# A graph layer with residual and layer norm: the first 1024 nodes' two halves take turns, group by group

## The chip, the cores and the metric

The kernel runs on one core of one Trainium2 chip. The metric is the device time of one execution in microseconds (us), the median of three runs. The core has engines that run side by side and meet through semaphores: TensorE (PE, matmuls; PEld are its weight loads), VectorE (DVE), ScalarE (ACT), GpSimd (POOL) and SyncE (SP), which here only starts transfers. ACT can start transfers as well, in a queue of its own.

## The reference

```python
support = x @ weight                                # x 4096 x 256, weight 256 x 256
h = (1.0 - ts) * support + ts * (adj @ support)     # adj 4096 x 4096, ts = t[0]
y = layernorm(x + h)                                # over the 256 features, eps 1e-5
```

Everything is float32. The kernel computes z = ts * (adj @ x) + (1 - ts) * x first and then z @ weight, which is the same sum with the large product taken first.

## The kernel before

The output nodes are cut into 8 chunks of 512 (`WIDE`). For one chunk the kernel needs all 32 blocks of 128 rows of x (`x_hi`, `x_lo`, 128 x 256 each, kept in SBUF once loaded) against the 32 blocks of that chunk's transposed adjacency (128 x 512 each, 256 KB). Four adjacency blocks form a group of 1 MB (`GROUP`), so a chunk has 8 groups; a group lives in one of four slots (`RING`) of `a_raw`, `a_hi` and `a_lo`.

Float32 products are made from two rounded parts. For each adjacency piece ACT writes the rounded high part `a_hi` (L209 for the first pieces, L216 for whole groups), DVE writes the rest `a_lo = a_raw - a_hi` (L370, L299), and PE then multiplies hi x hi, hi x lo and lo x hi (L449, L450, L451), for each of the two halves of the features (`k`): six matmuls of 512 columns for a block, 24 for a group. The blocks of x are split the same way: the first four by DVE (`x_hi`, L358) and POOL (`x_lo`, L273), the others by ACT (L203) and DVE (L364). The sums of a chunk stand in two PSUM banks `agg[c % 2]`.

While x is still coming, chunk 0 runs in small pieces (`PIECES`: first block, number of blocks), in the order in which they arrive: piece p is x blocks and adjacency blocks together. ACT's queue starts the first four adjacency pieces (L197), SP's queue the first five x pieces (L126), then x and adjacency in turn (L126, L131), and from block 16 on whole groups (L140). SP starts the load of a group into a slot when DVE has made `a_lo` of what stood there; ACT writes `a_hi` of a group when PE has used up the slot (`a_used`). So loading and splitting run up to four groups ahead of PE, and each engine follows the same written order of groups.

PE's own order is: 8 matmuls on zeros (`WARM`, L539), the first block (`first_piece`, L457 to L465), the pieces of chunk 0, its groups 4 to 7, and then for each next chunk group 0, the projection of the chunk before (`project`, 24 matmuls of 256 columns), and groups 1 to 7. `make_z` and `z_high` turn a finished chunk's `agg` into the operands `z_hi`, `z_lo` of that projection; they stand in DVE's and ACT's order ahead of the fourth group of the next chunk, and `layernorm` behind the fifth. The last chunk has a finish of its own (`project_last`).

## Time and profile before

| | us |
|---|---|
| median of 3 runs | 388.32 (387.94 to 388.32) |
| the profiled execution | 388.26 |
| its span, first to last instruction | 386.4 |
| PE busy / DVE busy / ACT busy / POOL busy | 377.9 / 226.7 / 145.5 / 20.7 |

The profiled execution took 388.26 us, of which 386.4 lie between its first and last instruction. Busy times are sums of an engine's instructions; a busy PE is not PE at its peak, since matmuls overlap. The distance from one matmul's start to the next is the figure to read. In the rows, `x8` is a number of instructions in one line, and in the timeline the brackets at the end give the idle time ahead of an instruction and what ended it.

### The profile page before, as it was taken

The numbers are of one execution on the slowest core, as the hardware profiler recorded it, in microseconds if no ns is written. First come the engines' busy times: TensorE is split into PE (matmuls) and PEld (weight loads), VectorE is DVE, ScalarE is ACT, GpSimd is POOL, SyncE is SP. The second block draws the span as 40 slices with busy tenths as digits, with TensorE's granted clock in tenths as the row PEclk, the third lists the DMA queues.
The fourth block names the chain that finished last, engine by engine and source line by source line (L and its number), as shares of the span: only waits on it lengthen the run. The fifth ranks groups of instructions, "written<-read, shape, count | busy, mean of one in ns | idle before, by whom it ended". The sixth has DMA issues, their size and how long they took to land.

```text
span 386.4 us, 4238 instructions
## 1 busy us (share of the span) xinstructions
PE 377.9 (98%) x1744; PEld 314.7 (81%) x1744; DVE 226.7 (59%) x292; ACT 145.5 (38%) x111; POOL 20.7 (5%) x20
## 2 busy tenths in 40 slices
PE   7999999999999999999999999999999999999993
PEld 5787888888888888888888888888888888888883
DVE  3978789454693356744576446763378444693115
ACT  4777553323523324233424325233333233523002
POOL 3200220010000100001000100001000010000000
PEclk9999999999999999999999999999999999999999
DMA  7999996566556565565646656647556565420001
GB/s 244 390 415 418 420 412 229 191 245 265 165 205 236 216 236 202 170 266 217 246 164 220 222 196 260 219 163 271 175 207 219 177 257 215 145 102 31 0 0 55
DMA packets 19251, 83.89 MB, mean 217 GB/s; under 512 B 1952, under 2 KB 7072, under 8 KB 11552
## 3 DMA queue, kind: packets, MB, share of 16 engines
...
q14 instruction: 6, 0.05, 0.0%
HBM read 79.43 MB, written 4.19 MB: 216 GB/s over the span
## 4 chain that ended last, share of the span: by engine, by line
PE 91%; DMA 5%; DVE 3%; ACT 1%; ACTq 0%; issue 0%; SPq 0%
PE agg L449 28%; PE agg L450 28%; PE agg L451 28%; DMA a_raw<-in_adjT 5%; PE out_ps L507 2%; PE out_ps L506 2%; PE out_ps L505 2%; DVE a_lo L370 1%; DVE a_lo L299 1%; ACT a_hi L216 0%; DVE x_lo L364 0%; DVE stats L419 0%; ACT x_raw L262 0%; ACTq L197 0%; ACT a_hi L209 0%
## 5 line engine op out<-in xcount | busy, mean ns | idle before, releaser
L299 DVE TENSOR_TENSOR a_lo<-a_raw,a_hi 128x2048 fp32r<-128x2048 f32 x60 | 140.8, 2348 | 123.2 <-ACT a_hi L216 123.2
L449 PE MATMUL agg<-a_hi,x_hi 128*128 128x512 f32 x510 | 199.0, 390 | 0.5 <-DVE a_lo L299 0.3
L450 PE MATMUL agg<-a_lo,x_hi 128*128 128x512 f32 x510 | 198.5, 389 | 0.0
L451 PE MATMUL agg<-a_hi,x_lo 128*128 128x512 f32 x510 | 198.4, 389 | 0.0
L216 ACT ACTIVATE a_hi<-a_raw 128x2048 fp32r<-128x2048 f32 x60 | 114.9, 1915 | 136.8 <-PE agg L451 127.7
L449 PEld LDWEIGHTS agg<-a_hi,x_hi 128*128 128x128 f32 x510 | 95.7, 188 | 21.8 <-DVE a_lo L370 1.3
L451 PEld LDWEIGHTS agg<-a_hi,x_lo 128*128 128x128 f32 x510 | 95.7, 188 | 20.1
L450 PEld LDWEIGHTS agg<-a_lo,x_hi 128*128 128x128 f32 x510 | 95.8, 188 | 19.4
L278 POOL TENSOR_TENSOR xt<-xt,omt_col 128x1024 f32<-128x1024 f32 x8 | 15.7, 1957 | 287.7 <-DMA xt<-in_xT 287.7
L223 ACT ACTIVATE z_hi<-z 128x512 fp32r<-128x512 f32 x14 | 8.9, 634 | 26.2 <-DVE z L312 26.2
L227 ACT ACTIVATE std<-var_eps 128x4 f32<-128x4 f32 x7 | 1.4, 205 | 42.1 <-DVE var_eps L335 42.1
L507 PE MATMUL out_ps<-w_hi,z_lo 128*128 128x256 f32 x56 | 15.8, 283 | 0.0
L506 PE MATMUL out_ps<-w_lo,z_hi 128*128 128x256 f32 x56 | 15.8, 283 | 0.0
L505 PE MATMUL out_ps<-w_hi,z_hi 128*128 128x256 f32 x56 | 15.8, 282 | 0.0
L370 DVE TENSOR_TENSOR a_lo<-a_raw,a_hi 128x512 fp32r<-128x512 f32 (+1 forms) x11 | 10.7, 972 | 3.7 <-ACT a_hi L209 3.3
L330 DVE BATCH_NORM_STATS2 stats<-x_raw 128x6 f32<-128x256 f32 x28 | 12.0, 428 | 1.0
L312 DVE SCALAR_TENSOR_TENSOR z<-agg,t_col,xt 128x512 f32<-128x512 f32 x14 | 10.4, 746 | 2.9 <-PE agg L451 2.9
L327 DVE TENSOR_TENSOR x_raw<-out_ps,rows 128x256 f32<-128x256 f32 x28 | 11.5, 410 | 0.0
L209 ACT ACTIVATE a_hi<-a_raw 128x512 fp32r<-128x512 f32 (+1 forms) x11 | 9.1, 828 | 5.4 <-DMA a_raw<-in_adjT 5.3
L505 PEld LDWEIGHTS out_ps<-w_hi,z_hi 128*128 128x128 f32 x56 | 10.7, 191 | 0.3
L506 PEld LDWEIGHTS out_ps<-w_lo,z_hi 128*128 128x128 f32 x56 | 10.7, 191 | 0.3
L507 PEld LDWEIGHTS out_ps<-w_hi,z_lo 128*128 128x128 f32 x56 | 10.7, 191 | 0.0
...
## 6 DMA issues: line engine op xcount, KB each, us to landing
...
x_raw<-in_x SPq DMA_DIRECT2D x5, 256.0 KB, 7.4
a_raw<-in_adjT ACTq DMA_DIRECT2D x4, 256.0 KB, 5.4
```

The lines of the kernel that those rows point to most:

```text
L216: nc.scalar.activation(a_hi[:, slot], a_raw[:, slot], ACT.Copy).then_inc(a_hi_ready[slot], 1)
L278: nc.gpsimd.tensor_tensor(xt[:, c % 2], xt[:, c % 2], omt_col[:, :].unsqueeze(2).broadcast_to([P, KT, WIDE]), ALU.mult).then_inc(xt_scaled, 1)
L299: nc.vector.tensor_tensor(a_lo[:, slot], a_raw[:, slot], a_hi[:, slot].bitcast(f32), ALU.subtract).then_inc(a_lo_ready[slot], 1)
L327: nc.vector.tensor_tensor(y_tile(i), out_ps[i][:, 0:feats], rows[:, c % 2, i], ALU.add).then_inc(y_ready[i], 1)
L330: nc.vector.bn_stats(stats[:, i], y_tile(i)).then_inc(stats_ready, 1)
L370: nc.vector.tensor_tensor(a_lo[:, j // GROUP, j % GROUP:j % GROUP + n], a_raw[:, j // GROUP, j % GROUP:j % GROUP + n], a_hi[:, j // GROUP, ...
L449: nc.tensor.matmul(bank, x_hi[:, j, cols], a_hi[:, slot, b], start=first, stop=False)
L450: nc.tensor.matmul(bank, x_hi[:, j, cols], a_lo[:, slot, b], start=False, stop=False)
L451: return nc.tensor.matmul(bank, x_lo[:, j, cols], a_hi[:, slot, b], start=False, stop=last)
L505: nc.tensor.matmul(dst, z_hi[:, k, cols], w_hi[:, k], start=(k == 0), stop=False)
L506: nc.tensor.matmul(dst, z_hi[:, k, cols], w_lo[:, k], start=False, stop=False)
L507: done = nc.tensor.matmul(dst, z_lo[:, k, cols], w_hi[:, k], start=False, stop=(k == KT - 1))
```

## The change

The order of the groups becomes one sequence n. For chunks 0 and 1 it alternates: n = 0 is chunk 0 group 0, n = 1 is chunk 1 group 0, n = 2 is chunk 0 group 1, and so on to n = 15; from n = 16 on it is chunk by chunk as before. The slot is n % 4. A group of x is thus used for two groups of adjacency in a row, and x is spread over the first 16 groups of work where it was spread over the first 8.

The pieces are cut anew. x has 12 pieces (`X_PIECES`: first block, count). The first four slots' adjacency has 13 pieces (`A_PIECES`: slot, first block, count, first and last column); slots 0 and 1 come block by block in turn, slots 2 and 3 in turns of two blocks. The first adjacency block comes as two transfers of 256 columns. ACT's queue starts pieces 0 to 3 (two halves, chunk 1's first block, chunk 0's second); SP's queue starts x 0, x 1, piece 4 (chunk 1's second block), x 2, pieces 5 and 6, x 3, and so on, with t and the weight behind all pieces. Splitting keeps to its engines: ACT `a_hi`, DVE `a_lo`, the first four x blocks by DVE and POOL.

PE runs 5 matmuls on zeros where it ran 8, and two more on zeros that write the banks of chunk 0; the first block follows as 12 matmuls of 256 columns where it was 6 of 512. The projection of chunk 0 comes behind n = 15, that of chunk 1 behind n = 18, the others where they were. `make_z`, `z_high`, `root` and `layernorm` keep their distances to the end of their chunk from chunk 2 on; for chunk 0 `make_z` stands ahead of n = 18 and `layernorm` behind n = 19, for chunk 1 ahead of n = 19 and behind n = 22. Loads of `xt` come two groups later, those of `rows` too from chunk 2 on, and the two that belong to chunk 0 come behind n = 8 and n = 10.

```diff
@@ -9,9 +9,12 @@
 GROUP = 4
 RING = 4
 X_RING = 3
-WARM = 8
-PIECES = ((0, 1), (1, 1), (2, 1), (3, 1), (4, 1), (5, 1), (6, 2), (8, 2), (10, 2), (12, 2), (14, 2),
-          (16, 4), (20, 4), (24, 4), (28, 4))
+WARM = 5
+X_PIECES = ((0, 1), (1, 1), (2, 1), (3, 1), (4, 2), (6, 2), (8, 4), (12, 4), (16, 4), (20, 4), (24, 4), (28, 4))
+A_PIECES = ((0, 0, 1, 0, 256), (0, 0, 1, 256, 512), (1, 0, 1, 0, 512),
+            (0, 1, 1, 0, 512), (1, 1, 1, 0, 512), (0, 2, 1, 0, 512), (1, 2, 1, 0, 512),
+            (0, 3, 1, 0, 512), (1, 3, 1, 0, 512),
+            (2, 0, 2, 0, 512), (3, 0, 2, 0, 512), (2, 2, 2, 0, 512), (3, 2, 2, 0, 512))
 EPS = 1e-5
 
 
@@ -27,11 +30,26 @@
     TILES = WIDE // P
     assert GROUPS == 2 * RING and KT == 2 and TILES == GROUP
 
-    EARLY = sum(first < GROUP for first, _ in PIECES)
-    RING_PIECES = sum(first < RING * GROUP for first, _ in PIECES)
-
-    def piece_after(blocks):
-        return sum(first < blocks for first, _ in PIECES)
+    EARLY = sum(first < GROUP for first, _ in X_PIECES)
+    SECOND = sum(first < 2 * GROUP for first, _ in X_PIECES)
+    A_EARLY = sum(slot < 2 for slot, *_ in A_PIECES)
+    TURNS = CHUNKS * GROUPS
+
+    def seq(c, g):
+        return 2 * g + c if c < 2 else c * GROUPS + g
+
+    def chunk_group(n):
+        return (n % 2, n // 2) if n < 2 * GROUPS else (n // GROUPS, n % GROUPS)
+
+    def x_after(blocks):
+        return sum(first < blocks for first, _ in X_PIECES)
+
+    def a_after(slot):
+        return max(q for q, piece in enumerate(A_PIECES) if piece[0] == slot) + 1
+
+    LAST = [seq(c, GROUPS - 1) for c in range(CHUNKS)]
+    PROJECT_AFTER = [LAST[c] + (3 if c == 1 else 1) for c in range(CHUNKS)]
+    NORM_AFTER = [PROJECT_AFTER[c] + 4 for c in range(CHUNKS)]
...
@@ -158,29 +184,37 @@
 
             load_x(0)
             load_x(1)
-            for p in range(2, len(PIECES)):
-                load_x(p)
-                if p >= 4 and p < RING_PIECES:
-                    load_adj_piece(p)
-                if p == 5:
-                    sp.dma_start(t_col[:, :], t.partition_broadcast(P)).then_inc(t_loaded, 16)
-                if p == 8:
-                    sp.dma_start(w_raw[:, :, :], W.rearrange("(k p) n -> p k n", p=P)).then_inc(w_loaded, 16)
-                if p >= RING_PIECES:
-                    load_adj(0, PIECES[p][0] // GROUP)
-            load_adj(1, 0)
-            load_xt(0)
-            load_rows(0)
-            for c in range(1, CHUNKS):
-                for g in range(1, GROUPS):
-                    load_adj(c, g)
-                    if g == 2:
-                        load_xt(c)
-                    if g == 5 and c + 1 < CHUNKS:
-                        load_rows(c)
-                if c + 1 < CHUNKS:
-                    load_adj(c + 1, 0)
-                store(c - 1)
+            load_adj_piece(4)
+            load_x(2)
+            load_adj_piece(5)
+            load_adj_piece(6)
+            load_x(3)
+            load_adj_piece(7)
+            load_adj_piece(8)
+            load_x(4)
+            load_adj_piece(9)
+            load_adj_piece(10)
+            load_x(5)
+            load_adj_piece(11)
+            load_adj_piece(12)
+            sp.dma_start(t_col[:, :], t.partition_broadcast(P)).then_inc(t_loaded, 16)
+            sp.dma_start(w_raw[:, :, :], W.rearrange("(k p) n -> p k n", p=P)).then_inc(w_loaded, 16)
+            for n in range(RING, TURNS):
+                c, g = chunk_group(n)
+                if c == 0:
+                    load_x(x_after(g * GROUP))
+                load_adj(n)
+                if c < 2 and g == 4:
+                    load_xt(c)
+                if c < 2 and g == 5:
+                    load_rows(c)
+                if c >= 2 and g == 4:
+                    load_xt(c)
+                if c >= 2 and g == 7 and c + 1 < CHUNKS:
+                    load_rows(c)
+                for d in range(CHUNKS - 1):
+                    if n == min(NORM_AFTER[d] + RING, TURNS - 1):
+                        store(d)
             c = CHUNKS - 1
             for i in range(2):
...
-                    if g == RING - 1:
-                        make_z(c - 1)
-                    a_low(c, g)
-                    if g == RING:
-                        layernorm(c - 1)
+            x_high(0)
+            a_low_piece(0)
+            a_low_piece(1)
+            x_high(1)
+            a_low_piece(2)
+            x_high(2)
+            a_low_piece(3)
+            a_low_piece(4)
+            x_high(3)
+            for q in range(5, A_EARLY):
+                a_low_piece(q)
+            for p in range(EARLY, SECOND):
+                x_low(p)
+                for q in (A_EARLY + 2 * (p - EARLY), A_EARLY + 2 * (p - EARLY) + 1):
+                    a_low_piece(q)
+            dve.wait_ge(w_hi_ready, 1)
+            nc.vector.tensor_tensor(w_lo[:, :, :], w_raw[:, :, :], w_hi[:, :, :].bitcast(f32), ALU.subtract
+                                    ).then_inc(w_lo_ready, 1)
+            dve.wait_ge(t_loaded, 16)
+            nc.vector.tensor_scalar(omt_col[:, :], t_col[:, :], -1.0, 1.0, ALU.mult, ALU.add).then_inc(omt_ready, 1)
+            for n in range(RING, TURNS):
+                c, g = chunk_group(n)
+                if c == 0:
+                    x_low(x_after(g * GROUP))
+                for d in range(CHUNKS - 1):
+                    if n == LAST[d] + RING:
+                        make_z(d)
+                a_low(n)
+                if n == 2 * GROUPS:
+                    dve.wait_ge(x0_lo_ready, EARLY)
+                    dve.wait_ge(x_lo_ready, len(X_PIECES) - EARLY)
+                for d in range(CHUNKS - 1):
+                    if n == NORM_AFTER[d]:
+                        layernorm(d)
             c = CHUNKS - 1
             dve.wait_ge(xt_scaled, c + 1)
...
+            def first_block():
+                def half(k, w, a, q):
+                    lo, hi = A_PIECES[q][3:]
+                    nc.tensor.matmul(agg[0][k][:, lo:hi], w[:, 0, k * P:(k + 1) * P], a_part(a, q)[:, 0],
+                                     start=False, stop=False)
+
                 pe.wait_ge(x0_hi_ready, 1)
-                pe.wait_ge(a0_hi_ready, 1)
-                for k in range(KT):
-                    nc.tensor.matmul(agg[0][k][:, :], x_hi[:, 0, k * P:(k + 1) * P], a_hi[:, 0, 0],
-                                     start=True, stop=False)
-                pe.wait_ge(a0_lo_ready, 1)
-                for k in range(KT):
-                    nc.tensor.matmul(agg[0][k][:, :], x_hi[:, 0, k * P:(k + 1) * P], a_lo[:, 0, 0],
-                                     start=False, stop=False)
-                pe.wait_ge(x0_lo_ready, 1)
-                for k in range(KT):
-                    nc.tensor.matmul(agg[0][k][:, :], x_lo[:, 0, k * P:(k + 1) * P], a_hi[:, 0, 0],
-                                     start=False, stop=False)
-
-            def piece(p):
-                j, n = PIECES[p]
-                pe.wait_ge(a0_lo_ready, p + 1)
-                if p < EARLY:
-                    pe.wait_ge(x0_lo_ready, p + 1)
+                for q in range(2):
+                    pe.wait_ge(a0_hi_ready, q + 1)
+                    for k in range(KT):
+                        half(k, x_hi, a_hi, q)
+                for q in range(2):
+                    pe.wait_ge(a0_lo_ready, q + 1)
+                    for k in range(KT):
+                        half(k, x_hi, a_lo, q)
+                    if q == 0:
+                        pe.wait_ge(x0_lo_ready, 1)
+                    for k in range(KT):
+                        half(k, x_lo, a_hi, q)
...
+
+            def piece(q):
+                slot, first, count, _, _ = A_PIECES[q]
+                c, g = chunk_group(slot)
+                pe.wait_ge(a0_lo_ready, q + 1)
+                if g == 0:
+                    pe.wait_ge(x0_lo_ready, first + 1)
                 else:
-                    pe.wait_ge(x_lo_ready, p - EARLY + 1)
-                for b in range(j, j + n):
+                    pe.wait_ge(x_lo_ready, x_after(g * GROUP + first + count) - EARLY)
+                for b in range(first, first + count):
+                    j = g * GROUP + b
                     for k in range(KT):
-                        done = products(0, b // GROUP, b, b % GROUP, k, False, False)
-                if (j + n) % GROUP == 0:
...
@@ -537,17 +581,18 @@
             pe.wait_ge(zeros_ready, 1)
             for _ in range(WARM):
                 nc.tensor.matmul(out_ps[0][:, :], z_hi[:, 0, 0:P], z_hi[:, 0], start=True, stop=True)
-            first_piece()
-            for p in range(1, RING_PIECES):
-                piece(p)
-            for g in range(RING, GROUPS):
-                group(0, g)
-            pe.wait_ge(w_lo_ready, 1)
-            for c in range(1, CHUNKS):
-                group(c, 0)
-                project(c - 1)
-                for g in range(1, GROUPS):
-                    group(c, g)
+            for k in range(KT):
+                nc.tensor.matmul(agg[0][k][:, :], z_hi[:, 0, 0:P], z_hi[:, 0], start=True, stop=False)
+            first_block()
+            for q in range(2, len(A_PIECES)):
+                piece(q)
+            for n in range(RING, TURNS):
+                group(n)
+                for d in range(CHUNKS - 1):
+                    if n == PROJECT_AFTER[d]:
+                        if d == 0:
+                            pe.wait_ge(w_lo_ready, 1)
+                        project(d)
             project_last()
 
 ```

ACT's loop has the same order as DVE's, with `a_high_piece`, `x_high`, `z_high` and `root` in the places of `a_low_piece`, `x_low`, `make_z` and `layernorm`; SP's `load_adj(n)` waits for the `a_lo` of the slot's last use as before.

## Rows read from the trace of the kernel before

**Rows 1.** The page: busy time of the engines, and GB/s in 40 slices.
```profile
PE 377.9 (98%) x1744; PEld 314.7 (81%) x1744; DVE 226.7 (59%) x292; ACT 145.5 (38%) x111; POOL 20.7 (5%) x20
...
GB/s 244 390 415 418 420 412 229 191 245 265 165 205 236 216 236 202 170 266 217 246 164 220 222 196 260 219 163 271 175 207 219 177 257 215 145 102 31 0 0 55
```
**Rows 2.** Waits of PE over the span: us in total, times, longest.
```profile
PE agg L457 <- ACT a_hi L209: 0.4, 1, 0.4
PE agg L449 <- DVE a_lo L299: 0.3, 1, 0.3
PE agg L449 <- DVE a_lo L370: 0.2, 1, 0.2
```
**Rows 3.** Timeline of PE at the start: start us, us, engine, line.
```profile
1.38 3.78 PE L539 MATMUL out_ps<-z_hi 128*128 128x512 f32 x8 [1.38 <-POOL z_hi L282]
5.56 1.09 PE L457 MATMUL agg<-a_hi,x_hi 128*128 128x512 f32 x2 [0.40 <-ACT a_hi L209]
6.49 0.63 PE L461 MATMUL agg<-a_lo,x_hi 128*128 128x512 f32 x2
...
7.76 0.50 PE L449 MATMUL agg<-a_hi,x_hi 128*128 128x512 f32 x1 [0.18 <-DVE a_lo L370]
8.10 0.40 PE L450 MATMUL agg<-a_lo,x_hi 128*128 128x512 f32 x1
...
9.33 0.50 PE L449 MATMUL agg<-a_hi,x_hi 128*128 128x512 f32 x1
...
18.05 0.39 PE L449 MATMUL agg<-a_hi,x_hi 128*128 128x512 f32 x1
...
28.25 0.39 PE L449 MATMUL agg<-a_hi,x_hi 128*128 128x512 f32 x1
...
29.42 0.50 PE L449 MATMUL agg<-a_hi,x_hi 128*128 128x512 f32 x1 [0.33 <-DVE a_lo L299]
```
**Rows 4.** Timeline of PE at the end of the last group.
```profile
376.26 0.28 PE L517 MATMUL out_ps<-w_hi,z_hi 128*128 128x256 f32 x1
376.38 0.28 PE L518 MATMUL out_ps<-w_lo,z_hi 128*128 128x256 f32 x1
```
**Rows 5.** Timeline of ACT: the pieces that waited, and the first whole group.
```profile
6.17 0.63 ACT L209 ACTIVATE a_hi<-a_raw 128x512 fp32r<-128x512 f32 x1 [0.76 <-DMA a_raw<-in_adjT]
7.67 0.63 ACT L209 ACTIVATE a_hi<-a_raw 128x512 fp32r<-128x512 f32 x1 [0.87 <-DMA a_raw<-in_adjT]
8.74 0.63 ACT L209 ACTIVATE a_hi<-a_raw 128x512 fp32r<-128x512 f32 x1 [0.44 <-DMA a_raw<-in_adjT]
...
25.12 1.92 ACT L216 ACTIVATE a_hi<-a_raw 128x2048 fp32r<-128x2048 f32 x1 [0.91 <-DMA a_raw<-in_adjT]
```
**Rows 6.** Timeline of DVE: the second and the third block's `a_lo`.
```profile
6.83 0.88 DVE L370 TENSOR_TENSOR a_lo<-a_raw,a_hi 128x512 fp32r<-128x512 f32 x1 [0.49 <-ACT a_hi L209]
...
8.33 0.94 DVE L370 TENSOR_TENSOR a_lo<-a_raw,a_hi 128x512 fp32r<-128x512 f32 x1 [0.42 <-ACT a_hi L209]
```
**Rows 7.** Timeline of the DMA queues: the starts of the first transfers.
```profile
0.80 2.28 SPq L126 DMA_DIRECT2D x_raw<-in_x  x5
0.81 1.85 ACTq L197 DMA_DIRECT2D a_raw<-in_adjT  x4
```
**Rows 8.** Transfers started at 1.24 us: KB each, us to landing.
```profile
a_raw<-in_adjT ACTq DMA_DIRECT2D x1, 256.0 KB, 4.9
x_raw<-in_x SPq DMA_DIRECT2D x1, 128.0 KB, 4.3
```
**Rows 9.** The same view, transfers started at 1.71 and 1.72 us.
```profile
a_raw<-in_adjT ACTq DMA_DIRECT2D x1, 256.0 KB, 5.9
x_raw<-in_x SPq DMA_DIRECT2D x1, 128.0 KB, 5.7
```
**Rows 10.** The page: groups of instructions, busy and mean ns, idle before.
```profile
L299 DVE TENSOR_TENSOR a_lo<-a_raw,a_hi 128x2048 fp32r<-128x2048 f32 x60 | 140.8, 2348 | 123.2 <-ACT a_hi L216 123.2
...
L312 DVE SCALAR_TENSOR_TENSOR z<-agg,t_col,xt 128x512 f32<-128x512 f32 x14 | 10.4, 746 | 2.9 <-PE agg L451 2.9
```

177 lines of the change are left out of this document (79 added, 98 removed).

## The prediction

> **What bounds the kernel now.** I read the page first: PE is busy 377.9 of 386.4 us, DVE 226.7 and ACT 145.5 [rows 1]. The waits of PE come next, and they are nearly nothing: three short ones on the product banks, 0.9 us together [rows 2]. So the kernel is a stream of matmuls, and the question is how dense the stream is. The timeline answers that. From 18.05 to 28.25 us 45 matmuls of 512 columns start, 0.2267 us apart [rows 3]; two of 256 columns start 0.12 us apart [rows 4]. From the first whole group at 29.42 us to the end of the last at 376.26 us there are 1440 of the wide ones and seven projections of 24 narrow ones: 1440 x 0.2267 + 168 x 0.12 = 346.6 us, and the rows give 346.84 [rows 3, 4]. Nothing is lost there. What can be won lies ahead of 29.42 us: from 5.56 us on 96 matmuls run, 21.76 us of work in 23.86 us, so 2.1 us are lost [rows 3]. Half of it goes before 9.33 us (12 matmuls, 2.72 us, in 3.77 us) and half behind (84 matmuls, 19.04 us, in 20.09 us). Ahead of 5.56 us PE waits for its first data.
>
> Both losses come from loading. The ACT rows say that each of the first pieces was split the moment it landed, at 6.17, 7.67 and 8.74 us [rows 5], and the first whole group at 25.12 us, when the queues moved 390 to 420 GB/s [rows 1, 5]; its matmuls were 0.49 us late, since the one before would have let them start at 28.93.
>
> **The later loss goes.** After the change a block of x and two adjacency blocks, 640 KB, feed twelve matmuls (2.72 us) where 768 KB did. Up to n = 4 the queues carry eight x blocks fewer, 1 MB, at 415 GB/s 2.5 us: the first whole group should land at 22.6 us for 25.12 now. ACT's 1.92 us [rows 5] and DVE's 2.35 us [rows 10] put it ready near 27 us with x's own splitting between, two us ahead of PE. DVE needs at most 0.94 us for a block's `a_lo` [rows 6] against PE's 1.36 us, so the splitting keeps ahead too. I take the 1.05 us behind the third block as gone but for 0.05 us.
>
> **The first block.** The half piece is a smaller transfer and should land some tenths earlier than the 256 KB one, and its `a_hi` is half the work. The first matmul comes near 4.9 us for 5.56. The zeros are 7 matmuls for 8, at the 0.45 us that those rows show (1.38 us on, eight in 3.78 us, the last one 0.63 long) they end in time [rows 3]. Twelve half matmuls cost 12 x 0.12 = 1.44 us for 6 x 0.2267 = 1.36: 0.08 us more, and twice that while the clock is still low. None of it counts if the block behind it is late, and it is: the first block should be through by 7 us.
>
> **The second and third piece** decide. They are the third and fourth transfer of ACT's queue (chunk 1's first block, chunk 0's second). ACT's queue holds 512 KB up to the second piece now and then, so by its own contents nothing changes. But the two queues share the engines. The transfers started at 1.24 us land 4.3 (x, 128 KB) and 4.9 us (adjacency, 256 KB) later, those of 1.71 and 1.72 us 5.7 and 5.9 us later [rows 8, 9]: the k-th transfer of one queue lands with the k-th of the other, though one is twice as large. All are 128 rows, one for each partition. Landed with the second pair (6.14 us) are 768 KB, with the third (7.62 us) 1152, with the fourth (8.70 us) 1536 [rows 5, 8, 9]; the starts are 0.46 us apart and bound nothing [rows 7]. After the change chunk 1's first block is third in its queue, and beside it SP's third is a whole adjacency block, not x. Together with the halves and x 0 and x 1, that is 1024 KB: 6.14 + 256/384 x 1.48 = 7.13 us. Chunk 0's second block is fourth, with 1408 KB: 7.62 + 256/384 x 1.08 = 8.34 us.
>
> The ends for the first of them: 6.14 us, if ACT's queue keeps its bytes per us, and 7.62 us, if the third pair lands when the third pair did. I take 7.13, between them by the bytes moved. From landing to the first matmul it was 7.76 - 6.14 = 1.62 us and 9.33 - 7.62 = 1.71 us [rows 3, 8, 9]. So PE starts chunk 1's first block at 8.75 us, a restart costs 0.11 us (8.10 - 7.76 = 0.34 for 0.23 us) [rows 3], and it is done at 8.75 + 1.36 + 0.11 = 10.22 us. The next is ready at 8.34 + 1.7 = 10.04 us, in time. At 10.22 us 12 blocks' worth of matmuls are done as at 9.33 us now, 0.89 us later, and behind it stand 84.
>
> **The rule weighed.** The landings in pairs are the row; a byte share of each queue would give other times. The Trainium skill (DMA: Bandwidth & Descriptors, Queues, rings and completion order) says that each DMA engine takes the queues in turn, a packet at a time. By strict turns the third transfer lands with the third pair, at 7.62 us. This speaks against the change, which puts larger transfers beside the ones that PE waits for. It is the second rival below.
>
> **The rest of the stream.** The projection of chunk 0 comes behind n = 15. Its operands need the end of n = 14, then `z` 0.75 us [rows 10], `z_hi` (0.63, the same shape as in rows 5) and `z_lo` (under 0.94, rows 6): 2.3 us beside 5.44 us of matmuls. Chunk 1's `z_hi` and `z_lo` wait for that projection (2.9 us behind n = 15), and behind them in ACT's and DVE's queues stand the splits of n = 19: ready at 2.9 + 1.3 + 0.9 + 1.9 + 2.35 = 9.4 us, needed after three groups and a projection, 22.1 us. Then `layernorm`: DVE's busy time without L299 is 85.9 us [rows 1, 10], at most 12.3 us for each of seven, so n = 20 is ready by 9.4 + 12.3 + 2.35 = 24.1 us, needed at 27.6. On SP's queue `xt` and `rows` move by two groups, with data that are wanted a chunk's end later. I count all this at nothing; without that cover a projection would cost its wait of up to 2.3 us. The last chunk is untouched.
>
> **Sum.** 10.22 + 84 x 0.2267 + 0.05 = 29.31 us for the start of the 97th block matmul, where it was 29.42: 0.1 us earlier. The profiled execution is 388.26 us, 0.06 under the median of 388.32; 388.26 - 0.1 gives **388.1 us** (388.16, the 0.05 for gaps being the most I allow). One loss goes and almost the same loss comes in ahead of it.
>
> **Rivals.** First, the pieces land by their place in ACT's queue: 6.14 and 7.62 us. PE starts them at 7.76 and 9.33 as now and only the later loss goes: 9.33 + 19.04 + 0.15 = 28.5 us, 0.9 us gained, **387.3 us**. For it speaks that early on the queues moved less than later (244 GB/s in the first slice for 415 [rows 1]), so room may be left for the larger rows; against it the landing in pairs.
>
> Second, strict turns: 7.62 us for chunk 1's first block. Start 9.33, done 10.8, 29.9 us, 0.5 us lost: **388.7 us**. Within 0.2% of now.
>
> Third, the clock, on the slower side. The matmuls on zeros start 0.45 us apart, those from 6.49 us on 0.23 us: PE went from its level of 1.2 GHz to that of 2.4 GHz around the first block, having run without a pause for 3.8 us and then with one of 0.4 us [rows 3]. After the change it has seven zeros, single half matmuls with waits between, and then stands still from about 7 to 8.75 us. If it is at the low level when chunk 1's first block begins, each matmul costs 0.22 us more: six cost 1.3 us, **389.4 us**, and this decides as soon as four or more run so. Against it: the pause of 0.4 us and the ones ahead of 7.76 and 9.33 us didn't bring it down now.
>
> Fourth, the turn of chunk 0 and 1 stalls PE behind n = 15 for over a us after all: 389 us and more.
>
> **How the numbers follow.** Forecast 0.40, by place 0.25, strict turns 0.18, clock 0.12, turn 0.05. A difference of 0.2% (0.78 us) is about what a measurement of this kernel can tell. Faster by more: most of the first rival and a tail of the forecast, 0.26. Slower by more: clock and turn, less their mild cases, 0.15. Within: 0.59. The range of 8 in 10 reaches from 387.2 (first rival, with 0.1 us of an earlier landing) to 389.0, with the second rival in and most of the clock out.
>
> **What would show it.** PE's first matmul near 4.9 us and the first block done by 7; then an idle of 1.5 to 2 us that ends with DVE's `a_lo` of chunk 1's first block, near 8.7 us; ACT's third piece starting at 7.1 us on a DMA. From about 10.2 us no idle of PE to the end, and the first whole group ready 2 us early. I am wrong on landing if ACT's third piece starts at 6.2 or at 7.7 us; on the clock if matmuls behind 8.7 us start over 0.4 us apart; on the cover if PE waits at the first narrow matmuls near 94 us.

## The result and the profile after

The changed kernel takes 390.65 us, the median of 10 runs (388.50 to 391.82), against 388.32 us for the kernel before, measured beside it (10 runs, 387.89 to 389.32). The ratio is 1.0051, with a 95% interval of 1.0036 to 1.0065: slower by 0.5%, and outside the predicted range, which ended at 389.0. The profiled execution took 390.79 us with a span of 389.1; that of before took 388.26 with a span of 386.4.

First the page of the changed kernel: its sums, and the GB/s of the 40 slices.

```profile
PE 379.9 (98%) x1749; PEld 317.7 (82%) x1749; DVE 224.5 (58%) x291; ACT 144.9 (37%) x110; POOL 21.4 (5%) x20
...
GB/s 227 368 416 417 416 411 255 184 168 222 142 252 277 170 263 188 245 216 201 212 238 207 187 254 217 224 207 202 227 166 271 175 202 271 145 101 26 0 0 56
```

PE is busy 2.0 us longer than before [rows 1], though there is hardly more to compute: the matmuls themselves have become slower somewhere. The first two slices carry less than before (227 for 244 and 368 for 390 GB/s). The waits of PE in the changed kernel (us in total, times, longest) don't name the loss:

```profile
PE out_ps L583 <- POOL z_hi L313: 1.4, 1, 1.4
PE agg L485 <- DVE a_lo L399: 0.6, 1, 0.6
PE agg L492 <- ACT a_hi L239: 0.6, 1, 0.6
```

The first of them, for the zeros at the very start, both kernels have. The two others are 1.2 us together, and before had 0.9 [rows 2]. The timeline of PE in the changed kernel (start us, us, engine, line) shows what the list of waits can't:

```profile
1.38 2.50 PE L583 MATMUL out_ps<-z_hi 128*128 128x512 f32 x5 [1.38 <-POOL z_hi L313]
3.68 1.05 PE L585 MATMUL agg<-z_hi 128*128 128x512 f32 x2
4.56 0.76 PE L492 MATMUL agg<-a_hi,x_hi 128*128 128x256 f32 x2
5.95 0.80 PE L492 MATMUL agg<-a_hi,x_hi 128*128 128x256 f32 x2 [0.62 <-ACT a_hi L239]
...
7.83 0.63 PE L492 MATMUL agg<-a_hi,x_lo 128*128 128x256 f32 x2
9.09 0.80 PE L485 MATMUL agg<-a_hi,x_hi 128*128 128x512 f32 x1 [0.63 <-DVE a_lo L399]
9.68 0.63 PE L486 MATMUL agg<-a_lo,x_hi 128*128 128x512 f32 x1
...
13.52 0.55 PE L486 MATMUL agg<-a_lo,x_hi 128*128 128x512 f32 x1
13.90 0.39 PE L487 MATMUL agg<-a_hi,x_lo 128*128 128x512 f32 x1
...
31.84 0.39 PE L485 MATMUL agg<-a_hi,x_hi 128*128 128x512 f32 x1
...
378.55 0.28 PE L561 MATMUL out_ps<-w_hi,z_hi 128*128 128x256 f32 x1
```

Wide matmuls that depend on nothing but the one before start 0.43 us apart up to 13.52 us, and 0.23 us apart from 13.90 on: PE stays at its level of 1.2 GHz for four microseconds of real work. In the kernel before the change to 0.23 us came with the first block, at about 6.5 us [rows 3]. From 9.09 to 13.90 us eleven matmuls take 4.81 us; at 0.2267 us, with the 0.11 us of a restart, they would take 2.60. That is **2.2 us, lost to the clock**. Behind it nothing is lost: the 97th block matmul starts at 31.84 us (29.42 before), the last group ends at 378.55, where the narrow matmuls behind it begin (376.26 before [rows 4]).

So 2.3 of the 2.7 us by which the span grew arise ahead of 31.84 us. The other 0.4 us lie behind the last group: from 378.55 us to the end of the span it is 10.5 us, from 376.26 us it was 10.1. The computing there is the same; the last wait of the kernel, SP's on the store of the result, is 2.4 us for 2.0.

The start of ACT in the changed kernel shows when the pieces landed, and so why PE had to wait:

```profile
4.00 0.42 ACT L239 ACTIVATE a_hi<-a_raw 128x256 fp32r<-128x256 f32 x1
5.48 0.42 ACT L239 ACTIVATE a_hi<-a_raw 128x256 fp32r<-128x256 f32 x1 [1.06 <-DMA a_raw<-in_adjT]
7.68 0.63 ACT L239 ACTIVATE a_hi<-a_raw 128x512 fp32r<-128x512 f32 x1 [1.78 <-DMA a_raw<-in_adjT]
8.68 2.19 ACT L239 ACTIVATE a_hi<-a_raw 128x512 fp32r<-128x512 f32 x4 [0.37 <-DMA a_raw<-in_adjT]
...
24.99 1.92 ACT L245 ACTIVATE a_hi<-a_raw 128x2048 fp32r<-128x2048 f32 x1 [1.44 <-DMA a_raw<-in_adjT]
```

The second half lands at 5.5 us, chunk 1's first block at 7.63 us, chunk 0's second at 8.6. Before, the next block was there at 6.14, the third at 7.62 [rows 5, 8, 9], and the whole first one by 4.78 us, as ACT's row of before shows:

```profile
4.78 0.63 ACT L209 ACTIVATE a_hi<-a_raw 128x512 fp32r<-128x512 f32 x1 [0.81 <-DMA a_raw<-in_adjT]
```

So the second half of the block came 0.7 us later than the whole block had. The third transfers of the two queues, as the view of transfers has them (KB each, us from issue to landing; they started at 1.71 and 1.73 us), land within 0.2 us of each other:

```profile
a_raw<-in_adjT SPq DMA_DIRECT2D x1, 256.0 KB, 5.8
a_raw<-in_adjT ACTq DMA_DIRECT2D x1, 256.0 KB, 5.9
```

### The profile page after: what moved, and what is told of

It is laid out like the page before. It is cut to its first block, busy times and chain, and to the rows that moved or that the text cites. A ratio compares the mean times of both kernels' runs of the same rounds, so it can differ in the third digit from the quotient of the medians.

```text
span 389.1 us, 4247 instructions
## 1 busy us (share of the span) xinstructions
PE 379.9 (98%) x1749; PEld 317.7 (82%) x1749; DVE 224.5 (58%) x291; ACT 144.9 (37%) x110; POOL 21.4 (5%) x20
## 3 DMA queue, kind: packets, MB, share of 16 engines
q10 hardware_dynamic: 864, 1.05, 1.1%
## 4 chain that ended last, share of the span: by engine, by line
PE 96%; DMA 2%; DVE 1%; ACT 1%; ACTq 0%; issue 0%
PE agg L485 30%; PE agg L486 30%; PE agg L487 30%; PE out_ps L551 2%; PE out_ps L550 2%; PE out_ps L549 2%; DMA a_raw<-in_adjT 2%; DVE stats L455 0%; ACT x_raw L293 0%; ACTq L230 0%; DVE a_lo L399 0%; ACT a_hi L239 0%; PE out_ps L561 0%; PE out_ps L563 0%; PE out_ps L562 0%; PE out_ps L567 0%
## 5 line engine op out<-in xcount | busy, mean ns | idle before, releaser
L330 DVE TENSOR_TENSOR a_lo<-a_raw,a_hi 128x2048 fp32r<-128x2048 f32 x60 | 138.6, 2311 | 124.3 <-ACT a_hi L245 124.3
L485 PE MATMUL agg<-a_hi,x_hi 128*128 128x512 f32 x510 | 199.6, 391 | 0.6 <-DVE a_lo L399 0.6
L486 PE MATMUL agg<-a_lo,x_hi 128*128 128x512 f32 x510 | 199.4, 391 | 0.0
L487 PE MATMUL agg<-a_hi,x_lo 128*128 128x512 f32 x510 | 199.1, 390 | 0.0
L245 ACT ACTIVATE a_hi<-a_raw 128x2048 fp32r<-128x2048 f32 x60 | 114.8, 1915 | 137.6 <-PE agg L487 134.1
L485 PEld LDWEIGHTS agg<-a_hi,x_hi 128*128 128x128 f32 x510 | 96.3, 189 | 20.7 <-DVE a_lo L399 0.9
L487 PEld LDWEIGHTS agg<-a_hi,x_lo 128*128 128x128 f32 x510 | 96.3, 189 | 20.3
L486 PEld LDWEIGHTS agg<-a_lo,x_hi 128*128 128x128 f32 x510 | 96.4, 189 | 19.6
L309 POOL TENSOR_TENSOR xt<-xt,omt_col 128x1024 f32<-128x1024 f32 x8 | 16.7, 2089 | 298.5 <-DMA xt<-in_xT 298.5
L399 DVE TENSOR_TENSOR a_lo<-a_raw,a_hi 128x512 fp32r<-128x512 f32 (+2 forms) x13 | 11.5, 903 | 5.9 <-ACT a_hi L239 5.5
L343 DVE SCALAR_TENSOR_TENSOR z<-agg,t_col,xt 128x512 f32<-128x512 f32 x14 | 10.4, 747 | 2.8 <-PE agg L487 2.8
L239 ACT ACTIVATE a_hi<-a_raw 128x512 fp32r<-128x512 f32 (+2 forms) x13 | 9.2, 727 | 7.2 <-DMA a_raw<-in_adjT 7.2
L349 DVE TENSOR_TENSOR z_lo<-z,z_hi 128x512 fp32r<-128x512 f32 x14 | 9.5, 687 | 2.8 <-ACT z_hi L252 2.2
L550 PEld LDWEIGHTS out_ps<-w_lo,z_hi 128*128 128x128 f32 x56 | 10.7, 191 | 0.3
L549 PEld LDWEIGHTS out_ps<-w_hi,z_hi 128*128 128x128 f32 x56 | 10.7, 191 | 0.3
## 6 DMA issues: line engine op xcount, KB each, us to landing
a_raw<-in_adjT SPq DMA_DIRECT2D x5, 256.0 KB, 6.8
x_raw<-in_x SPq DMA_DIRECT2D x4, 128.0 KB, 4.7
```

The costliest lines, as they stand in the source:

```text
L245: nc.scalar.activation(a_hi[:, slot], a_raw[:, slot], ACT.Copy).then_inc(a_hi_ready[slot], 1)
L309: nc.gpsimd.tensor_tensor(xt[:, c % 2], xt[:, c % 2], omt_col[:, :].unsqueeze(2).broadcast_to([P, KT, WIDE]), ALU.mult).then_inc(xt_scaled, 1)
L330: nc.vector.tensor_tensor(a_lo[:, slot], a_raw[:, slot], a_hi[:, slot].bitcast(f32), ALU.subtract).then_inc(a_lo_ready[slot], 1)
L399: nc.vector.tensor_tensor(a_part(a_lo, q), a_part(a_raw, q), a_part(a_hi, q).bitcast(f32), ALU.subtract).then_inc(a0_lo_ready, 1)
L485: nc.tensor.matmul(bank, x_hi[:, j, cols], a_hi[:, slot, b], start=first, stop=False)
L486: nc.tensor.matmul(bank, x_hi[:, j, cols], a_lo[:, slot, b], start=False, stop=False)
```

## The experiments

All times are medians in us, and each ratio is against the kernel before on the same chip in the same session. The kernel before had 388.28 (29 runs) beside the first four, 388.50 (25) beside the next four, 388.31 (27) beside the four after those and 388.57 (23) beside the last four.

| label | kernel | us (lowest to highest, runs) | ratio, 95% interval |
|---|---|---|---|
| e1_fill | after, zeros in both pauses | 389.05 (388.50 to 389.30, 11) | 1.0015, 1.0006 to 1.0023 |
| e2_before_w5 | before, 5 zeros for 8 | 388.61 (387.81 to 389.95, 12) | 1.0008, 0.9996 to 1.0019 |
| e3_x_first | after, all early x ahead on SP | 390.22 (388.77 to 390.68, 6) | 1.0042, 1.0026 to 1.0058 |
| e4_whole | after, first block whole | 388.44 (387.91 to 389.20, 12) | 1.0003, 0.9994 to 1.0011 |
| e5_warm8 | after, 8 zeros for 5 | 389.18 (388.38 to 391.13, 11) | 1.0019, 1.0008 to 1.0031 |
| e6_swap_fill | e1, chunk 1's first block by SP | 389.69 (389.04 to 390.91, 7) | 1.0035, 1.0022 to 1.0047 |
| e7_before_fill | before, two more zeros | 388.39 (388.06 to 388.97, 11) | 0.9999, 0.9990 to 1.0008 |
| e8_before_halves | before, first block in halves | 390.23 (389.44 to 391.67, 6) | 1.0050, 1.0032 to 1.0069 |
| e9_layout | after, adjacency stored in order of use | 391.92 (391.19 to 392.08, 4) | 1.0086, 1.0073 to 1.0100 |
| e10_before_far | before, two early blocks from far away | 388.52 (387.88 to 388.80, 11) | 1.0001, 0.9992 to 1.0009 |
| e11_whole_fill | e4 and 8 zeros | 388.26 (387.70 to 389.64, 11) | 1.0003, 0.9993 to 1.0013 |
| e12_whole_fill_layout | e11, stored in order of use | 387.52 (387.33 to 387.98, 11) | 0.9977, 0.9968 to 0.9986 |
| e13_halves_fill_layout | e1, stored in order of use | 389.64 (389.42 to 390.10, 5) | 1.0032, 1.0020 to 1.0044 |
| e15_after_again | after, once more | 389.43 (388.74 to 390.68, 7) | 1.0027, 1.0014 to 1.0039 |
| e16_best_again | e12, once more | 387.54 (387.20 to 388.15, 10) | 0.9981, 0.9972 to 0.9990 |
| e17_whole_layout | e12 with 5 zeros | 388.47 (387.69 to 389.65, 11) | 1.0002, 0.9991 to 1.0013 |

### The clock: zeros in the pauses

Theory: PE's two pauses, behind the first half and behind the first block, keep it at 1.2 GHz. The edit leaves every transfer and every wait and lets PE multiply zeros into an idle bank where it would stand still.

```diff
 pe.wait_ge(a0_hi_ready, q + 1)
 for k in range(KT):
     half(k, x_hi, a_hi, q)
+if q == 0:
+    fill(2)       # two 512-column matmuls on zeros into out_ps[0]
 ...
 first_block()
+fill(2)
```

> The changed kernel with four more matmuls on zeros, 512 columns each: two behind the first half's matmuls and two behind the first block, in the two pauses of 0.6 us that PE has there; nothing else differs. Theory (clock): these pauses keep PE at its low level until 13.8 us, which costs 2.2 us; filled, the spacing goes from 0.43 to 0.23 us before 9 us, the 97th block matmul starts near 29.6 us for 31.84, and the time is 388.4 to 388.8 us. Rival (landing): the time is lost because chunk 1's first block lands 1.5 us later than the second piece of the kernel before did; fillers don't change that and the time stays at 390.5 us or rises by up to 0.4.

Measured 389.05 us, ratio 1.0015, for 1.0051 of after and 1.0027 of its second series (below). PE at the start of this kernel:

```profile
6.55 0.50 PE L496 MATMUL agg<-a_hi,x_hi 128*128 128x256 f32 x2 [0.38 <-ACT a_hi L239]
6.89 0.40 PE L496 MATMUL agg<-a_lo,x_hi 128*128 128x256 f32 x2
...
9.32 0.50 PE L485 MATMUL agg<-a_hi,x_hi 128*128 128x512 f32 x1 [0.84 <-DVE a_lo L399]
9.66 0.40 PE L486 MATMUL agg<-a_lo,x_hi 128*128 128x512 f32 x1
```

The level comes up at about 6.5 us, as before, and the matmuls of chunk 1's first block start 0.23 us apart, 0.84 us of pause notwithstanding. The kernel does four matmuls more and ends earlier. But it still stands above the kernel before, and not by its clock: the last group ends 0.5 us later than in before (376.77 us), and from there to the end it is 10.7 us for 10.1.

The change also takes three of the eight zeros away at the start. Given back in after:

```diff
-WARM = 5
+WARM = 8
```

> The changed kernel with 8 matmuls on zeros ahead of everything, as the kernel before had, for 5; nothing else differs. They and the two that write the banks end near 5.7 us, so the pause of 0.6 us ahead of the second half is closed, the one of 0.6 to 0.8 us ahead of chunk 1's first block stays. Theory (clock): closing the first pause is enough for the spacing to fall to 0.23 us before 8 us, as with the fillers in both pauses: 388.8 to 389.3 us. Rival (both pauses count): 390 to 390.7 us, with the low level past 10 us.

389.18 us, ratio 1.0019, and the level is up by 7.6 us: the same as with the fillers. The other way round, the kernel before with five zeros:

> The kernel before with 5 matmuls on zeros for 8, so that PE pauses for 1.2 us more ahead of its first block; loads and splits are untouched. Theory (clock): the pause alone keeps the low level beyond 9 us, each of the matmuls until it rises costs 0.2 us more, the time is 389.5 to 391 us and differs between runs by over 1 us. Rival (landing): no load or split depends on these matmuls, so the time stays at 388.3 us.

388.61 us, where I had expected 389.5 or more. PE pauses 1.8 us ahead of 5.68 us and then stays at 0.43 us until 10.9 us, and yet little is lost. The third block's matmuls start 1.6 us later than in before (10.94 for 9.33), the first whole group's only 0.6 us later (30.04 for 29.42): the 1.05 us that PE loses there in before, waiting for loads, are gone, so most of the slow matmuls run inside waiting time. The number of zeros alone is not what made after slow. And more zeros don't help the kernel before:

```diff
-WARM = 8
+WARM = 9
 ...
 first_piece()
+nc.tensor.matmul(out_ps[0][:, :], z_hi[:, 0, 0:P], z_hi[:, 0], start=True, stop=True)
```

> The kernel before with 9 matmuls on zeros for 8 and one more behind the first block, in its pauses of 0.4 and 0.2 us; nothing else differs. Theory (clock): the kernel before too loses some of its time to a low level in part of its executions, which is why its times reach from 387.7 to 388.9 us; without a pause the level rises early in all of them: median 388.0 us and a spread under 0.6 us. Rival (its spread comes from loading): 388.3 to 388.5 us with the same spread.

388.39 us, the same as before.

After itself came out at 388.5 to 391.8 us, a wider spread than the kernel before has. So it was profiled once more, with nothing changed:

> The changed kernel itself, unchanged, for a second profile. Theory (a property of the order of the transfers): chunk 1's first block again lands between 7.5 and 8 us, the queues again move under 250 GB/s from 4 to 6 us, PE pauses twice for over 0.5 us before 9.5 us, and the low level lasts past 9 us: 390.0 to 391 us. Rival (the first profile was a chance): landing near 7.1 us and over 270 GB/s.

This profiled execution took 389.15 us. Its PE:

```profile
5.91 0.80 PE L492 MATMUL agg<-a_hi,x_hi 128*128 128x256 f32 x2 [0.60 <-ACT a_hi L239]
...
8.74 0.79 PE L485 MATMUL agg<-a_hi,x_hi 128*128 128x512 f32 x1 [0.33 <-DVE a_lo L399]
9.33 0.63 PE L486 MATMUL agg<-a_lo,x_hi 128*128 128x512 f32 x1
9.76 0.62 PE L487 MATMUL agg<-a_hi,x_lo 128*128 128x512 f32 x1
10.19 0.43 PE L485 MATMUL agg<-a_hi,x_hi 128*128 128x512 f32 x1
10.46 0.40 PE L486 MATMUL agg<-a_lo,x_hi 128*128 128x512 f32 x1
```

The same kernel and the same pause behind the first half, a shorter one ahead of chunk 1's first block (0.33 us for 0.63), and the level is up at 10.2 us and not at 13.8. Three matmuls are slow where eleven were: from 8.74 to 10.19 us 1.45 us for 3 x 0.2267 + 0.11 = 0.79, so 0.7 us lost to the clock and not 2.2. The last group ends at 376.69 us, 1.86 earlier than in the first execution: 1.5 us of it are the clock's and 0.35 the earlier start of chunk 1's first block. What the change costs depends on the execution.

### The halves alone

Two kernels take the halves apart from the rest of the change. In after, the first block whole again (one piece, six 512-column matmuls; ACT's queue carries the same three blocks in three transfers, SP's queue is unchanged, and the chunks still take turns):

```diff
-A_PIECES = ((0, 0, 1, 0, 256), (0, 0, 1, 256, 512), (1, 0, 1, 0, 512),
+A_PIECES = ((0, 0, 1, 0, 512), (1, 0, 1, 0, 512),
 ...
```

> The changed kernel with the first adjacency block as one transfer of 256 KB and six matmuls of 512 columns, so that chunk 1's first block is the second transfer of ACT's queue; SP's queue and the turns of the chunks are kept. Theory (turns): chunk 1's first block lands near 6.2 us and chunk 0's second near 7.7 us, as the second and third piece of the kernel before; the first block starts near 5.5 us, chunk 1's at 7.8 us, and the pauses ahead of them add up to under 1.3 us with 7 zeros ending at 4.5 us. With the clock up by 8 us the time is 387.4 to 388 us, below the kernel before; if the clock stays low as in the changed kernel it is 389.5 to 390. Rival (the turns of the chunks themselves cost the 2.3 us): 390.5 us.

388.44 us: no difference from before, though PE pauses 1.47 us ahead of 6.20 us and is slow until 10.1 us. Chunk 1's first block, second in ACT's queue again, landed at 7.0 us, not near 6.2 as expected. With eight zeros as well:

> The changed kernel with the first adjacency block whole, and 8 zeros for 5, so that PE has no pause of 1.5 us ahead of it. Against the same kernel with 5 zeros (388.44 us): theory (clock) the low level ends by 8 us for 10.1, three or four matmuls of the stream that sets the end are 0.2 us shorter each: 387.7 to 388.1 us. Rival (the loads bind up to 10 us): 388.4 us.

388.26 us. The turns of the two chunks, with all that they move, come out even. They lose 1.0 us in front (the 13th block matmul starts at 10.35 us for 9.33) and win 0.85 us behind it (from there to the 97th it is 19.24 us for 20.09). And the halves put into the kernel before, with nothing else of the change:

```diff
-for p in range(4):
+act.dma_start(a_raw[:, 0, 0:1, 0:256], adjT[0, :, 0:1, 0:256]).then_inc(half_loaded, 16)
+act.dma_start(a_raw[:, 0, 0:1, 256:512], adjT[0, :, 0:1, 256:512]).then_inc(a0_loaded[0], 16)
+for p in range(1, 4):
     load_adj_piece(p)
 ...
```

> The kernel before with one part of the change alone: the first adjacency block as two transfers of 256 columns, split in two and multiplied as twelve matmuls of 256 columns behind two that write zeros (6 + 2 zeros in all, for 8). Theory (the halves take a place in ACT's queue): the second piece lands as the third transfer, at 7.3 to 7.7 us for 6.15, the pauses grow, and the time is 389 to 390.5 us. Rival (only the turns of the chunks and SP's larger transfers delay it): the second piece lands at 6.2 us and the time is 388.0 to 388.4 us.

390.23 us, 1.7 us more than before, between the 2.3 us of after's first series and the 0.9 us of its second. One part of the change, put in alone, costs about what the whole does, but not by the path that I had expected. The profile is of the slowest of its six executions, 391.67 us. The second piece, now the third transfer of ACT's queue, was to land at 7.3 to 7.7 us. ACT in it, at that piece:

```profile
6.50 0.63 ACT L218 ACTIVATE a_hi<-a_raw 128x512 fp32r<-128x512 f32 x1 [1.09 <-DMA a_raw<-in_adjT]
```

That is 0.3 us later than in before [rows 5], and PE starts on it at 7.90 us for 7.76. ACT again, at the x blocks ahead of the first whole group and at that group:

```profile
23.10 1.06 ACT L204 ACTIVATE x_hi<-x_raw 128x1024 fp32r<-128x1024 f32 x1 [0.21 <-DMA x_raw<-in_x]
...
26.99 1.92 ACT L225 ACTIVATE a_hi<-a_raw 128x2048 fp32r<-128x2048 f32 x1 [2.30 <-DMA a_raw<-in_adjT]
```

and PE, from the last early piece on:

```profile
28.96 0.39 PE L469 MATMUL agg<-a_hi,x_lo 128*128 128x512 f32 x1
31.28 0.64 PE L467 MATMUL agg<-a_hi,x_hi 128*128 128x512 f32 x1 [1.93 <-DVE a_lo L310]
31.72 0.63 PE L468 MATMUL agg<-a_lo,x_hi 128*128 128x512 f32 x1
...
34.71 0.49 PE L469 MATMUL agg<-a_hi,x_lo 128*128 128x512 f32 x1
35.04 0.39 PE L467 MATMUL agg<-a_hi,x_hi 128*128 128x512 f32 x1
```

The pieces near the start came nearly in time (the third block's matmuls begin at 9.73 us for 9.33). What is late is the first whole group, at 26.99 us where it was 25.12 [rows 5], and PE pauses 1.9 us for it. Then the clock adds to it: behind that pause eight matmuls start 0.43 us apart, 8 x 0.2 = 1.6 us more.

Of the 1.9 us, 0.5 are there already at the x blocks (23.10 us for 22.63). The other 1.4 arise in the group's own load: it lands 3.9 us behind them, in before 2.5. The view of transfers of e8 from 23.5 to 24.9 us names the one thing in that load that before doesn't have there, a packet of a queue of its own (packets, MB, share of the 16 engines):

```profile
q8 instruction: 1, 0.02, 4.9%
```

In before such a packet falls between 26 and 26.5 us, in the second whole group's load, and that group is there 4.8 us behind the first (29.91 for 25.12 us). That the packet holds the load up is likely, and not shown: e10 below has one at the same time, and its second group comes 3.9 us behind the first. So the profiled execution shows a late group and the clock, and what half a block at the front of ACT's queue costs by itself stays open in this kernel; the other five executions, 389.44 us at the least, have no profile.

### The landing of chunk 1's first block

Theory after e1: it lands late since SP's queue has a whole adjacency block beside it where there was x. The edit puts all early x blocks ahead on SP.

```diff
 load_x(1)
+load_x(2)
+load_x(3)
 load_adj_piece(4)
-load_x(2)
 load_adj_piece(5)
 load_adj_piece(6)
-load_x(3)
```

> The changed kernel with SP's queue in the order x 0, x 1, x 2, x 3, then pieces 4, 5 and 6; nothing else differs. Theory (turns): the third transfer of one queue lands with the third of the other, so chunk 1's first block has 128 KB less beside it and lands near 7.2 us for 7.65, chunk 0's second block 0.3 us earlier than now; PE starts at 8.6 us for 9.09. Its pauses get shorter, so the clock may rise earlier: 388.5 to 390.3 us. Rival (place in its own queue): landing at 7.65 us as before and 390.6 us.

390.22 us, and chunk 1's first block landed at 7.8 us, not earlier than 7.63. With 128 KB beside it for 256 the third transfer of ACT's queue gained nothing, against the theory of bytes. But the pair came apart: x 2, the third transfer of SP's queue, landed at 6.9 us, 0.9 us ahead. And the queues moved 139 GB/s from 4 to 6 us for 210, so the run isn't a clean test of either. If the place in the queue counts, the block has to get another place:

```diff
 load_x(0)
+load_adj_piece(2)
 load_x(1)
 ...
-for q in range(4):
+for q in (0, 1, 3):      # ACT's queue; with the fillers of e1
```

> The changed kernel with the four fillers, and chunk 1's first block started by SP as its second transfer for ACT as its third; ACT's queue has the halves and chunk 0's second block. Theory (place in its queue and what stands ahead in both): chunk 1's first block lands at 6.0 to 6.8 us for 7.9, PE starts it at 7.7 to 8.4 us for 9.3, chunk 0's second block lands at 7.6 us and is the next to wait for: 387.4 to 388.2 us. Rival (the queues as a whole deliver too little by then, in whatever order): landing past 7.3 us and 388.8 to 389.2 us.

389.69 us. The block landed at 6.3 us, in the second place of SP's queue, 1.6 us earlier than in e1 (7.9). But x 1, moved back by a place, slipped from 5.6 to 8.8 us, the second half from 6.1 to 6.5, chunk 0's second block from 8.9 to 9.3. PE started chunk 1's first block at 9.81 us, and that isn't the block's landing any more. DVE in this run:

```profile
8.87 0.29 DVE L390 CAST x_hi<-x_raw 128x256 fp32r<-128x256 f32 x1 [1.47 <-DMA x_raw<-in_x]
9.07 0.68 DVE L400 TENSOR_TENSOR a_lo<-a_raw,a_hi 128x512 fp32r<-128x512 f32 x1
```

In DVE's written order `x_high(1)` stands ahead of the block's `a_lo`, so DVE waited for x 1, which this block doesn't need. The pairs hold here (6.3 and 6.5 us, 8.8 and 9.3), and an early place is paid for by what is moved back; with DVE's order changed as well the run might have ended otherwise, and that wasn't tried.

### Place in memory, and the best kernel

From 4 to 6 us the queues moved 312 GB/s in the kernel before and 210 in after. Two rows of the view by windows (us, busy us and instructions of each engine, clock, DMA share, GB/s), the first of before:

```profile
4.00:6.00 2.00, 1.60 (x4) 0.81 (x4) 0.85 (x2) 0.63 (x1) 0.73 (x1) 1.00 0.98 312
```

and the second of after:

```profile
4.00:6.00 2.00, 1.38 (x5) 0.56 (x4) 0.49 (x2) 0.83 (x2) 0.39 (x1) 1.00 0.86 210
```

After reads two places of the adjacency by turns, eight groups (8 MB) apart. Is that the cause? In after, the groups stored in the order in which they are used:

```diff
-return adjT[c * GROUPS + g, :, b:b + n, lo:hi]
+return adjT[slot, :, b:b + n, lo:hi]
 ...
+order = [(n % 2) * groups + n // 2 if n < 2 * groups else n for n in range(chunks * groups)]
+adjT = adjT[np.array(order)]
```

> The changed kernel with the transposed adjacency stored in DRAM in the order in which the groups are used, so that chunk 1's first group stands 1 MB behind chunk 0's first and not 8 MB. Same transfers, same sizes, same order. Theory (place in memory): the kernels that read chunk 1 in the first 2 us move 140 to 210 GB/s between 4 and 6 us where the others move 284 to 312; near by, it is over 270 again, chunk 1's first block lands near 6.5 us for 7.65, and the time falls by 1 to 1.5 us, to 389.2 to 389.7. Rival (the count of transfers and rows in the two queues): the place doesn't matter, landing at 7.6 us, 390.5 us.

391.92 us, the slowest of all. From 4 to 6 us it moved 137 GB/s. But its PE is the clearest view of the clock in this study:

```profile
5.81 0.50 PE L492 MATMUL agg<-a_hi,x_hi 128*128 128x256 f32 x2 [0.61 <-ACT a_hi L239]
6.15 0.40 PE L492 MATMUL agg<-a_lo,x_hi 128*128 128x256 f32 x2
...
9.70 0.79 PE L485 MATMUL agg<-a_hi,x_hi 128*128 128x512 f32 x1 [2.44 <-DVE a_lo L399]
10.29 0.63 PE L486 MATMUL agg<-a_lo,x_hi 128*128 128x512 f32 x1
...
14.56 0.63 PE L487 MATMUL agg<-a_hi,x_lo 128*128 128x512 f32 x1
14.99 0.48 PE L485 MATMUL agg<-a_hi,x_hi 128*128 128x512 f32 x1
```

Here the level had come up by 5.8 us (pairs of half matmuls 0.24 us apart), and the pause of 2.44 us took it down again, for twelve matmuls. So what the storage costs in this kernel (1.3 us and more against after) is in part clock. With the fillers in those pauses and the same storage:

> The changed kernel with the four fillers and the adjacency stored in the order of use, the halves kept. With the whole first block and fillers the same order of storage gave 387.5 us, with halves and no fillers 391.9 us. Theory (halves): the two transfers of 256 columns take two places in ACT's queue whatever the order of storage, chunk 1's first block lands at 7.6 us or later, and a pause of over 1 us stays ahead of it: 388.8 us or more. Rival (only the low clock made the halves costly): 387.5 to 388.0 us.

389.64 us: chunk 1's first block starts at 9.68 us as in e9, the level stays up, and the time is 2.3 us below e9's. Then the kernel before, whose second and fourth piece are read from chunk 1's first group (which is the wrong adjacency for two of its blocks, at the same work):

> The kernel before, whose second and fourth adjacency piece are read from chunk 1's first group, 8 MB away, in place of chunk 0's; sizes, queues and everything else are kept (chunk 0's sums so take the wrong adjacency in two of 32 blocks). Theory (place in memory): 4 to 6 us falls from 312 to 200 GB/s or less, the second piece lands at 7 us or later for 6.14, and the time rises to 389 to 390.5 us. Rival (count of transfers): unchanged, 388.4 us.

388.52 us, pieces landing at 6.13 and 7.42 us as ever, 313 GB/s from 4 to 6 us. Far places alone cost nothing, so they don't explain the dip. Last, the storage in order of use with the block whole and eight zeros:

> As the run with the whole first block and 8 zeros, and the adjacency stored in the order of use. If both the place in memory and the pause cost time, chunk 1's first block lands at 6.2 to 6.5 us, PE runs without a wait from 7.9 us on, and the time is 387.0 to 387.6 us, below the kernel before. Rival (the place doesn't matter): the same as without the new order.

387.52 us, 0.23% less than before; and once more:

> The same kernel as e12_whole_fill_layout: turns of the chunks, the first block whole, 8 zeros, storage in the order of use. A second measurement: 387.4 to 387.7 us against 388.3 of the kernel before, an interval below 1. If it was a chance, the ratio is 1 within 0.001.

387.54 us, 0.19% less. PE in it:

```profile
6.18 1.17 PE L491 MATMUL agg<-a_hi,x_hi 128*128 128x512 f32 x2 [0.17 <-ACT a_hi L239]
7.17 0.65 PE L491 MATMUL agg<-a_lo,x_hi 128*128 128x512 f32 x2
7.66 0.62 PE L491 MATMUL agg<-a_hi,x_lo 128*128 128x512 f32 x2
8.38 0.50 PE L484 MATMUL agg<-a_hi,x_hi 128*128 128x512 f32 x1
```

From 8.38 us on there is no wait to the end; the last group ends at 375.63 us for 376.26. The same kernel with five zeros:

> As e16_best_again with 5 zeros for 8: the changed kernel with the whole first block and storage in the order of use. Theory (clock): PE pauses for 1 us or more ahead of its first block, the low level lasts to about 10 us, and the time is 387.9 to 388.4 us. Rival (the pause costs nothing as the loads bind up to 10 us): 387.5 us.

388.47 us: a pause of 1.3 us ahead of 6.03, PE slow until 10.4 us, and 0.9 us lost. In this kernel the zeros are worth what they were not worth in the kernel before (e2). And e13 against e16, both with the level up, both stored in order of use, differ by the halves: 389.64 to 387.54, 2.1 us, of which 0.6 us lies in the tail (10.7 us from the last group to the end for 10.1). Without that storage it is e1 against e11: 0.8 us, half of it in the tail (10.7 for 10.3).

## Why the prediction was wrong

**The bound and the place of the losses: right.** All of the difference up to the tail arose ahead of the first whole group; behind it PE is as dense as it was (346.7 us from 31.84 to 378.55, 346.84 in before).

**The first block: right in its start, wrong in its end.** The first half matmul ran at 4.56 us (forecast 4.9). But the block was through at 8.5 us, not by 7: I took the second half to be there at once, and it landed at 5.5 us, 1.7 us behind the first; and the remaining ten ran at 1.2 GHz. The step "none of it counts if the block behind it is late" left out that here a pause cost twice, as time and as a level. A waiting PE was taken for free time. In after's first series that was the largest loss: e1 and e5, which fill pauses and change nothing else, take most of it away.

**The landing: off by 0.5 us, and no rule of mine holds.** In the profiled execution chunk 1's first block came at 7.63 us for 7.13, the second rival's time, and started at 9.09 for 8.75, only 0.34 us late, since landing to start took 1.46 us for 1.62 (DVE's part 0.69 us for 0.88 and 0.94 [rows 6]). In the second profiled execution it landed at 7.31 and started at 8.74. Pairs fit after (7.5 and 7.6 us) and e6, not e3 (6.9 and 7.8 us). Places in a queue don't fit e8, where the second piece, third in ACT's queue, landed at 6.5 us for 6.1 as second, nor e4, where a second transfer landed at 7.0 us. My interpolation by bytes fits e8 (6.6 us) and misses after, e3 and e4. The rule of the Trainium skill that I had weighed (DMA: Bandwidth & Descriptors, Queues, rings and completion order), queues served in turn a packet at a time, goes with the landings in pairs where they are found, and by itself it doesn't give e8's 6.5 us. I had written that "by its own contents nothing changes" since ACT's queue holds 512 KB up to that piece either way. It holds one transfer more, and in the kernels whose chunks take turns the block landed at 7.3 us or later with the halves (after, e1, e3, e5, e9, e13, e15) and between 6.1 and 7.2 us without them (e4, e11, e12, e16, e17). The halves delay it there; by what mechanism stays open.

**The clock: the step that failed.** The sum put it at nothing, and the third rival, which had it, was mis-sized and given too small a chance. It was priced at six slow matmuls, 1.3 us, and ended at 389.4; there were eleven in one execution (2.2 us) and three in the other (0.7 us), and the ten halves ahead of them at 0.43 a pair. My reason against it was the pause of 0.4 us in before, which didn't bring the level down. But that pause ended at 5.56 us and the level came up at about 6.5 us, so there was none to bring down: only the 0.18 us ahead of 7.76 us were a pause at the high level. What the rows said is that eight zeros and a pause of 0.40 us let the level rise by 6.5 us. The change has seven zeros, the first half's two matmuls and a pause of 0.62 us, and there it rose at 13.8 and at 10.2 us. In e1 and e5, which only add matmuls on zeros, the level was up by 6.5 and 7.6 us and the ratio fell from 1.0051 and 1.0027 to 1.0015 and 1.0019. The Trainium skill (TensorE: Matmul & The Clock Gate, What's actually happening) has it that the low level is the default, which activity lifts; the start of every kernel here agrees (0.43 to 0.45 us apart at first in all of them), and the rule would have pointed at the zeros taken away and the pauses put in.

**The later loss goes: right.** There is no wait of PE behind 9.09 us. In the first profiled execution the group did not come 2.5 us earlier, as forecast; it landed at 24.99 us for 25.12, behind two small pieces for which ACT waited 1.5 and 1.0 us at 12.4 and 14.0 us, and the wait vanished since PE arrived 2.4 us later, at 31.84. But in the second execution it came when the forecast had it:

```profile
22.63 1.92 ACT L245 ACTIVATE a_hi<-a_raw 128x2048 fp32r<-128x2048 f32 x1 [1.42 <-DMA a_raw<-in_adjT]
```

In e1 it was 23.33 us. In the best kernel, e16, it is 22.78 us, PE is early (8.38 us), and there is no wait either, so the cover is real.

**The turn: right.** No wait near 94 us: in after the projection of chunk 0 begins at 97.12 us, directly behind the last matmul ahead of it (96.89), and e4 and e11 equal the kernel before within their intervals. The fourth rival fell.

**The tail was not in the sum.** The store of the result takes 0.4 us longer at the end in after and in e1, e3, e5, e9, e13 and e15, and not in those with a whole block, nor in e8 and e6, which have the halves too: there the tail is 10.1 and 10.3 us. So it isn't the halves alone. The sum took it as unchanged. I have no cause for it.

By terms, from the forecast 388.16 to the profiled 390.79: landing 0.34, clock 2.2 (together 2.53 for the 97th block matmul, 31.84 for 29.31), tail 0.4, and -0.3 for a stream 0.13 us shorter and 0.17 us less around the span. That is the first execution; the median's 390.65 is close to it, but the second series of the same kernel came out at 389.43.

**What stays open.** Why the early transfers slow down: from 4 to 6 us 210 GB/s in after (221 in its second execution), 170 in e1, 132 to 139 in e3, e9 and e13, 199 in e4 and 204 in e11, against 299 to 313 in before, e2, e7, e10, e12 and e16. Part of it is only when the bytes move: from 2 to 4 us after carried 251 GB/s where before carried 187, so that up to 6 us it is behind by 7% and not by a third. Not the distance in memory alone (e10), not adjacency blocks in place of x ahead on SP (e3), and storage in order of use lifts it with a whole block (e11 to e12, 204 to 299) and not with halves (e1 to e13, 170 to 132). Neither do I know what the halves cost in the kernel before without the late group of the profiled execution (e8), nor what makes the level rise at 10.2 us in one execution and at 13.8 in another of the same kernel.
